# Mamba-2 block and FFN on one core: own decays on four row groups, past decays split into two factors, y between the two projections

## The chip, the core and the metric

The kernel is one program on one core of one Trainium2 chip. The metric is the device time of one execution in microseconds. Six engines are named by the profile: PE (TensorE matmuls), PEld (TensorE weight loads), DVE (VectorE), ACT (ScalarE), POOL (GpSimd) and SP (SyncE, which here only issues DMAs). They run their own instruction streams in order and meet through semaphores.

## The reference, cut to what matters

The input is x of shape (4, 256, 512). Two residual blocks follow each other: a Mamba-2 block (in-projection, causal convolution of length 4, a decayed attention-like sum over two chunks of 128 tokens, gate, group norm, out-projection) and a quantised FFN. The change lies in the first:

```python
# b=4 batches, s=256 tokens, chunks of 128; H=128 heads of P=64; G=8 groups; N=128; K=4
gate, hBC, dt = split(layernorm(x) @ in_proj_w.T)        # 8192 | 8192+2*1024 | 128
hBC = silu(causal_conv(hBC) + conv_b)                    # hs (8192), Bm (8*128), Cm (8*128)
dt  = clip(softplus(dt + dt_bias), 0, 100);  A = -exp(A_log)
xch = hs * dt                                            # per head
A_cum = cumsum(dt * A) within a chunk
L = exp(segsum(dt * A))                                  # L[l,s] = exp(A_cum[l]-A_cum[s]), s <= l
Y_diag = einsum(C, B, L, xch)                            # a chunk on itself ("own")
states = einsum(B, exp(A_cum[last] - A_cum), xch)        # left behind by a chunk
Y_off  = einsum(C, states of the chunk before, exp(A_cum))   # second chunk on the first ("past")
y = Y_diag + Y_off + hs * D
g = y * silu(gate);  out = groupnorm(g) * norm_w @ out_proj_w.T
```

With two chunks per batch, each head needs three decay matrices of 128x128 per batch: chunk 0 on itself, chunk 1 on the past chunk 0, chunk 1 on itself.

## The kernel before

The 1024 tokens lie on the free axis. The 8192 channels are 64 tiles of 128 channels (two heads each), eight tiles per group. `step(g, j, par_, ...)` exists once for every engine and does tile j of group g; `over_tiles` runs it 64 times, with two parities `par_`, and after each eight tiles `window(g, nxt)`, which projects the next group's B and C, multiplies them (`cbs`), takes the group norm's sums and does the out-projection of the group. The FFN (`over_chunks`) comes last. Inside a step TensorE also projects the channels of the NEXT tile, in four units `unit(0)` to `unit(3)`: inputs for tokens 0 to 511 and 512 to 1023, then gate for the same halves. A unit is twelve matmuls of 512 columns (fp32 split into an upper and a lower part, L758 to L760). `unit` waits on `split` (weights ready) and `taken` (the bank of the unit before is read out).

What TensorE does in a step before: `turn(0)` (four transposes of the tile's inputs, L858), `exponents(0)`, `exponents(1)`, `unit(0)`, `turn(1)`, `exponents(2)`, `exponents(3)`, `unit(1)`, `y_first` (8 matmuls, L881), `exponents(4)`, `exponents(5)`, `unit(2)`, `unit(3)`, `y_second` (16 matmuls, L891). `exponents(q)` (L867) is one bf16 matmul over rows of three exact parts of the cumulative sums; it leaves A_cum[l]-A_cum[s] for one kind (q // 2: own 0, past, own 1) and one head (q % 2) in one of three PSUM banks (`diff0`, `diff1`, `misc`).

ScalarE turns these into decays: Relu with scale -1 and Exp with scale -1 for the own kinds (L640, L644), a plain Exp for the past (L634). VectorE multiplies with C·B (`weigh`, L1163, into M), multiplies the transposed inputs with dt (`times_dt`, L1155), runs the last three taps of the convolution (`conv_rest`, L1068), the silu products (`hs_silu` L1082, `gate_silu` L1087), and adds y to the skip term (L1189, which signals `ysum`). ScalarE also does the first tap (`tap3`, L558), the tanh of inputs (`hs_tanh`, L569) and gate (`gate_tanh`, L573), the rounding of the raw weights to their upper part (`upper_pair`, L536, waits for `s_raw`), and scale and rounding of the out-projection's weights (L666, L672). GpSimd makes the lower parts (L406, L430), gated = y * gate (L438), its squares (L447) and their sum (L452). SP loads, per step, the raw out-projection weights (`wo_raw`), the rows of the next tile (`load_rows`, one DMA of `row_r` and three of `row_l`), and two raw weight pieces (`load_pair`).

The order on each engine is the order in which the code is written; nothing reorders it. The same small pool of PSUM banks (two `proj`, two `diff`, two `y`, `trb`, `misc`) ties the engines together.

Of the kernel before, what the change touches and what calls it, by code (L numbers as in the profile page):

```python
# [5 lines left out]
F32 = mybir.dt.float32  # L6
F32R = mybir.dt.float32r
BF16 = mybir.dt.bfloat16
ALU = mybir.AluOpType
# [20 lines left out]
UNITS = 6  # L30
SLOT = [0, 1, 2, 3, 0, 1]
# [18 lines left out]
def over_tiles(eng, step, window):  # L50


    with eng.Fori(0, G - 1) as g:
        with eng.Fori(0, TPG // 2) as p:
            step(g, 2 * p, 0, True, True)
            step(g, 2 * p + 1, 1, True, True)
        window(g, True)
    with eng.Fori(0, TPG // 2 - 1) as p:
        step(G - 1, 2 * p, 0, True, True)
        step(G - 1, 2 * p + 1, 1, True, True)  # L60
    step(G - 1, TPG - 2, 0, True, False)
    step(G - 1, TPG - 1, 1, False, False)
    window(G - 1, False)
# [12 lines left out]
def mamba_ffn(nc, x, win, wdt, par, parbc, dt_bias, a_log, wout, w1, w3, w2, s1, s3, s2, out):  # L76
    rows_r = nc.dram_tensor("rows_r", (3, H, TOK), BF16, kind="Internal").ap()
    rows_l = nc.dram_tensor("rows_l", (3, B, H, 3, P), BF16, kind="Internal").ap()

    with ExitStack() as ctx:  # L80
# [23 lines left out]
        M = sb("M", [P, 4, HALF])  # L104
        bc = M[:, :, :].rearrange("p (a u) f -> p a (u f)", a=2)
# [3 lines left out]
        row_r = sb("row_r", [P, 2, 2, TOK], BF16)  # L109
        row_l = sb("row_l", [P, 2, 2, 3 * P], BF16)  # L110
        sq = sb("sq", [P, 2, HALF])
        after, bias_bc, nega_bc = [sq[:, 0, i * P:(i + 1) * P] for i in range(3)]
# [12 lines left out]
        qs = sb("qs", [P, 2, 4])  # L125
        qr = sb("qr", [P, 2, 4])
# [9 lines left out]
        rev, revrem = dte[:, 0:HALF], dte[:, HALF:TOK]  # L136
        r_part = flat[:, 4 * TOK:6 * TOK].bitcast(BF16)[:, 0:3 * TOK].rearrange("p (k f) -> p k f", k=3)
        neg_part = flat[:, 6 * TOK:8 * TOK].bitcast(BF16)[:, 0:3 * TOK].rearrange("p (k f) -> p k f", k=3)
        rev_part = pre[0].bitcast(BF16)[:, 0:3 * HALF].rearrange("p (k f) -> p k f", k=3)
# [3 lines left out]
        f_pair = M[:, :, :].rearrange("p k (w f) -> p w k f", w=2)  # L143
# [27 lines left out]
        dbank = diff + [misc]  # L171
# [32 lines left out]
        s_part = [sem(f"exact_part{k}") for k in range(3)]  # L204
        s_rest = sem("rest_of_parts")
        s_rows = sem("rows_stored")
        s_raw = [sem("w_raw0_loaded"), sem("w_raw1_loaded")]
        s_rowq = [sem("rows_even_loaded"), sem("rows_odd_loaded")]
        s_out = sem("out_stored")
# [10 lines left out]
        turned = Tally(sem("hs_transposed"), 0, 2)  # L220
        xdts = Tally(sem("xdt_done"), 1, 2)
        dready = Tally(sem("diff_ready"), 0, UNITS)
        dbound = Tally(sem("diff_bounded"), 0, 4)
        edone = Tally(sem("exp_done"), 0, UNITS)
        mdone = Tally(sem("decay_done"), 3, UNITS)
        yready = Tally(sem("y_ready"), 1, 3)
# [47 lines left out]
        def _(sp):  # L274
# [12 lines left out]
            for n in range(3):  # L287
                load_pair(n, 2 * n if n else None)

            def load_rows(t, par_):  # L290
                sp.dma_start(row_r[0:3, par_, :, :], rows_r[:, bass.ds(2 * t, 2), :]).then_inc(s_rowq[par_], 16)
                for k in range(3):
                    sp.dma_start(row_l[3 + 4 * k:7 + 4 * k, par_, :, :].rearrange("b h f -> b (h f)"),
                                 rows_l[k, :, bass.ds(2 * t, 2), :, :].rearrange("b h q f -> b (h q f)"))\
                        .then_inc(s_rowq[par_], 16)


            for k in range(3):
                sp.wait_ge(s_part[k], 3)
                sp.dma_start(rows_r[k, :, :], r_part[:, k, :]).then_inc(s_rows, 16)  # L300
                sp.dma_start(rows_l[k, :, :, 1, :].rearrange("b h l -> h b l"),
                             rev_part[:, k, :].rearrange("h (b l) -> h b l", b=B)).then_inc(s_rows, 16)
                for z in range(2):
                    sp.dma_start(rows_l[k, :, :, 2 * z, :].rearrange("b h l -> h b l"),
                                 neg_part[:, k, :].rearrange("h (b z l) -> h z b l", z=2, b=B)[:, z, :, :])\
                        .then_inc(s_rows, 16)
            sp.wait_ge(s_const, 13)
            sp.dma_start(row_r[3:15, 0, 1, :], row_r[3:15, 0, 0, :]).then_inc(s_marks, 16)
            sp.dma_start(row_r[3:15, 1, 0, :], row_r[3:15, 0, 0, :]).then_inc(s_marks, 16)
            sp.dma_start(row_r[3:15, 1, 1, :], row_r[3:15, 0, 0, :]).then_inc(s_marks, 16)  # L310
            sp.wait_ge(s_rows, 16 * 12)
            load_rows(0, 0)

            def step(g, j, par_, nxt, nxt2):
# [39 lines left out]
        def _(pool):  # L354
# [18 lines left out]
            e.memset(row_r[:, :, :, :], 0.0).then_inc(s_const, 1)  # L373
            e.memset(row_l[:, :, :, :], 0.0).then_inc(s_const, 1)
            pool.wait_ge(s_const, 9)
            e.memset(row_l[0:3, :, :, :], 1.0).then_inc(s_const, 1)
            columns = row_r[:, 0, 0, :].rearrange("p (b f) -> p b f", b=B)
            for k in range(3):
                pool.wait_ge(s_const, 10 + k)
                e.affine_select(out=columns, in_=columns, compare_op=ALU.not_equal, fill=1.0, base=-3 - 4 * k,  # L380
                                pattern=[[-1, B], [0, S]], channel_multiplier=1).then_inc(s_const, 1)
# [31 lines left out]
            split_pair(0, 0)  # L413
            split_pair(1, 2)

            wholes = ((acum, rem, r_part), (rev, revrem, rev_part))
            for i, (whole, rest, parts) in enumerate(wholes):
                pool.wait_ge(s_part[0], i + 1)
                e.tensor_tensor(rest, whole, parts[:, 0, :], ALU.subtract).then_inc(s_rest, 1)
            for i, (whole, rest, parts) in enumerate(wholes):  # L420
                pool.wait_ge(s_rest, i + 1)
                pool.wait_ge(s_part[1], i + 1)
                e.tensor_tensor(parts[:, 2, :], rest, parts[:, 1, :], ALU.subtract).then_inc(s_part[2], 1)
            split_pair(1, 4)

            def step(g, j, par_, nxt, nxt2):
# [15 lines left out]
                for h in range(2 if nxt else 0):  # L442
                    pool.wait_ge(gdone.sem, gdone.at(g, j, h + 1))
# [907 lines left out]
```

## Time and profile before

| | us |
|---|---|
| median of 3 runs | 1861.39 (1861.02 to 1861.64) |
| the profiled execution | 1863.36 |
| its span on the core | 1861.6 |
| PE busy | 1805.1 (97%) |
| DVE busy | 1256.5 (67%) |
| POOL busy | 1006.2 (54%) |
| ACT busy | 918.5 (49%) |
| mean granted TensorE clock | 0.986 of full speed |

The span is what the core's trace covers; 1.8 us of the profiled execution lie around it, and that execution is 1.97 us above the median. The matmuls' ends are modelled, so that a busy PE is no proof that the array has no gaps: the chain of waits is read for that.

### The profile page before, as it was taken

Reading aid. Unit: us, or ns where it says so; the run is one execution under the profiler, and the core shown is the slowest. Engines: PE = TensorE matmul, PEld = TensorE weight load, DVE = VectorE, ACT = ScalarE, POOL = GpSimd, SP = SyncE. Lnnn points to the kernel's source line nnn. Section 1 sums busy time; section 2 is a strip of 40 time slices with the busy share of each in tenths; the row PEclk is TensorE's granted clock in tenths of the full one; section 3 lists DMA queues with packets and bytes.
Section 4 is the critical chain, followed back from the end, with each engine's and each line's share of the span. In section 5 each row is a group of like instructions: output and inputs, shape, how many; then the busy total and the mean of one; then the engine's idle time right before and its main releaser. Section 6 shows DMA issues by size and latency. Waiting matters only on the chain.

```text
span 1861.6 us, 35838 instructions
## 1 busy us (share of the span) xinstructions
PE 1805.1 (97%) x10520; PEld 1448.8 (78%) x10520; DVE 1256.5 (67%) x2147; ACT 918.5 (49%) x1660; POOL 1006.2 (54%) x812
## 2 busy tenths in 40 slices
PE   5799999999999999999999999999999998999998
PEld 4577887788777877787778777887788776788886
DVE  6588728872887377746884688457754884877776
ACT  4466526652665256635663566346644663222221
POOL 4266645664566446654665366546654657633430
PEclk9899999999999999999999999999999997999999
DMA  2211101110111011101120111001101111111101
GB/s 93 63 53 41 46 3 45 52 52 0 47 53 52 0 47 51 53 0 36 46 64 6 29 53 53 17 29 53 47 23 30 42 35 53 40 52 35 51 17 46
DMA packets 49019, 74.94 MB, mean 40 GB/s; under 512 B 10356, under 2 KB 18676, under 8 KB 48984
## 3 DMA queue, kind: packets, MB, share of 16 engines
q1 hardware_dynamic: 47976, 73.12, 12.9%
q10 hardware_dynamic: 1008, 1.38, 0.2%
q8 instruction: 18, 0.29, 0.1%
q14 instruction: 17, 0.14, 0.0%
HBM read 70.35 MB, written 4.06 MB: 40 GB/s over the span
## 4 chain that ended last, share of the span: by engine, by line
PE 94%; DVE 2%; POOL 1%; issue 1%; ACT 1%; POOLq 0%; DVEq 0%; ACTq 0%
PE proj L758 16%; PE proj L760 16%; PE proj L759 16%; PE y L891 7%; PE y L945 6%; PE y L947 6%; PE y L946 6%; PE y L881 4%; PE trb L858 3%; PE diff L867 3%; PE y L758 2%; PE y L760 2%; PE y L759 2%; PE misc L867 1%; PE misc L931 1%
## 5 line engine op out<-in xcount | busy, mean ns | idle before, releaser
L758 PE MATMUL proj<-xhi,w_hi 128*128 128x512 f32 x1088 | 466.1, 428 | 5.4 <-DVE v L1068 5.4
L760 PE MATMUL proj<-xhi,w_lo 128*128 128x512 f32 x1088 | 426.2, 392 | 0.0
L759 PE MATMUL proj<-xlo,w_hi 128*128 128x512 f32 x1088 | 425.5, 391 | 0.0
L406 POOL TENSOR_TENSOR w_lo<-w_raw,w_hi 128x512 fp32r<-128x512 f32 x144 | 184.1, 1297 | 227.5 <-ACT w_hi L536 227.5
L1068 DVE SCALAR_TENSOR_TENSOR v<-proj,par_sb,v 128x510 f32<-128x510 f32 (+2 forms) x384 | 282.1, 742 | 14.9 <-ACT v L558 11.6
L758 PEld LDWEIGHTS proj<-xhi,w_hi 128*128 128x128 f32 x1088 | 205.0, 188 | 75.5 <-issue 7.9
L462 POOL TENSOR_TENSOR g_lo<-gated,g_hi 128x512 fp32r<-128x512 f32 x128 | 163.8, 1283 | 182.1 <-ACT g_hi L689 182.0
L760 PEld LDWEIGHTS proj<-xhi,w_lo 128*128 128x128 f32 x1088 | 204.8, 188 | 46.5
L759 PEld LDWEIGHTS proj<-xlo,w_hi 128*128 128x128 f32 x1088 | 205.4, 189 | 38.6
L1163 DVE TENSOR_TENSOR M<-diff,cb 128x512 f32<-128x512 f32 x256 | 170.4, 686 | 82.2 <-ACT diff L644 82.2
L945 PE MATMUL y<-wo_hi,g_hi 128*128 128x512 f32 x512 | 202.9, 396 | 4.0 <-POOL g_lo L462 4.0
L430 POOL TENSOR_TENSOR wo_lo<-wo_raw,wo_hi 128x512 f32 (+1 forms) x64 | 81.9, 1279 | 225.1 <-ACT wo_hi L672 225.1
L946 PE MATMUL y<-wo_lo,g_hi 128*128 128x512 f32 x512 | 200.1, 391 | 0.0
L947 PE MATMUL y<-wo_hi,g_lo 128*128 128x512 f32 x512 | 200.0, 391 | 0.0
L689 ACT CAST g_hi<-gated 128x512 fp32r<-128x512 f32 x128 | 78.6, 620 | 233.6 <-PE y L947 233.6
L558 ACT ACTIVATE v<-proj,par_sb 128x512 f32<-128x512 f32 x128 | 99.6, 778 | 188.7 <-PE proj L760 188.7
L1207 DVE SCALAR_TENSOR_TENSOR resid<-y,rg,resid 128x512 f32<-128x512 f32 x64 | 48.0, 750 | 201.3 <-PE y L947 171.5
L640 ACT ACTIVATE diff<-diff 128x512 f32<-128x512 f32 x192 | 105.5, 579 | 138.1 <-PE diff L867 138.1
L438 POOL TENSOR_TENSOR gated<-hs,gate 128x512 f32 (+1 forms) x128 | 162.8, 1295 | 1.6 <-DVE hs L1189 1.6
L452 POOL TENSOR_TENSOR sqacc<-sqacc,sq 128x512 f32<-128x512 f32 x128 | 163.1, 1297 | 0.0
L891 PEld LDWEIGHTS y<-M,xdt 128*64 128x64 f32 x2048 | 112.0, 138 | 25.7 <-issue 22.2
L891 PE MATMUL y<-M,xdt 128*64 128x128 f32 x2048 | 127.6, 278 | 2.5 <-DVE M L1163 2.5
(179 smaller groups left out, 3420.1 us busy)
## 6 DMA issues: line engine op xcount, KB each, us to landing
w_raw<-in_win SPq DMA_DIRECT2D x144, 256.0 KB, 2.7
wo_raw<-in_wout SPq DMA_DIRECT2D x64, 256.0 KB, 2.6
M<-in_w SPq DMA_DIRECT2D x14, 512.0 KB, 3.7
cb<-in_w SPq DMA_DIRECT2D x7, 512.0 KB, 3.4
row_l<-rows_l SPq DMA_DIRECT2D x192, 6.0 KB
out<-resid SPq DMA_DIRECT2D x8, 256.0 KB, 2.0
rows_l<-gated SPq DMA_DIRECT2D x9, 128.0 KB, 2.5
resid<-in_x SPq DMA_DIRECT2D x4, 256.0 KB, 4.7
```

Source lines behind the costliest of these rows:

```text
L406: e.tensor_tensor(w_lo[:, slot, i, :], w_raw[:, i, :], w_hi[:, slot, i, :].bitcast(F32), ALU.subtract).then_inc(split.sem, 1)
L452: e.tensor_tensor(halves(sqacc, h), halves(sqacc, h), sq[:, h, :], ALU.add)\
L462: e.tensor_tensor(g_lo[:, kk, :, :], gated[:, 4 * kk:4 * kk + 4, t * P:(t + 1) * P], g_hi[:, kk, :, :].bitcast(F32), ALU.subtract).then_in ...
L758: e.matmul(o, hi_l, hi_r, start=first, stop=False)
L759: e.matmul(o, hi_l, lo_r, start=False, stop=False)
L760: return e.matmul(o, lo_l, hi_r, start=False, stop=last)
L891: mm = e.matmul(ybank[b // 2][head * HD:(head + 1) * HD, (b % 2) * S + P:(b % 2 + 1) * S], xdt[:, 2 * b + part, head * HD:(head + 1) * HD] ...
L945: e.matmul(o, g_hi[:, kk, k, :], wo_hi[:, kt, :], start=first, stop=False)
L946: e.matmul(o, g_hi[:, kk, k, :], wo_lo[:, kt, :], start=False, stop=False)
L947: mm = e.matmul(o, g_lo[:, kk, k, :], wo_hi[:, kt, :], start=False, stop=last)
L1068: e.scalar_tensor_tensor(dst[:, :, d:S], src[:, :, 0:S - d], weights(K - 1 - d), dst[:, :, d:S], ALU.mult, ALU.add)\
L1163: e.tensor_tensor(M[:, SLOT[q], :], dbank[q % 3][:, :], cb[:, q // 2, :], ALU.mult)\
```

## The change

Tiles, projections, window and FFN stay as they are. What changes:

- **Own exponents.** The rows of z (0, 1: own kinds) and head go to four groups of 15 partitions, at 0, 32, 64 and 96 (`first = 32 * (2 * z + head)`). `exponents(g, j, par_)` issues four matmuls of 512 columns, each contracting its own 15 rows, into the four banks of `decay[0]` and `decay[1]`. ScalarE and VectorE then work on two banks at once (1024 columns): two Relu, two Exp, two products per step in place of four, four and four.
- **Past decays.** No exponent matmul and no Exp any more. exp(A_cum[l]) is made once for all heads (`faded`, in DRAM) and loaded per tile as `fade_l` by two DMAs that broadcast a row to 128 partitions; GpSimd multiplies it with C·B into M[:, 4:6] (`weigh_past`, 1024 columns). The other factor, `fade_s` = exp(sum after s) * dt, is multiplied into a second copy of the transposed inputs, `xfade`, by VectorE.
- **Order.** A step starts with `unit(0)`, then all eight transposes in one go into the two y banks, `unit(1)`, all 24 matmuls of `y`, `exponents` of the NEXT tile, `unit(2)`, `unit(3)`. ScalarE's weight casts (`upper_pair`) move ahead of the second first tap, the out-projection's weights ahead of the decays, and the next tile's decays stand among the tanhs; VectorE adds y before the last silu products. The exponents of a group's first tile move into the window.
- **Rows.** `load_rows` issues eight DMAs (3 or 12 rows each) in place of four; `load_fade` adds two of 256 KB, behind a wait for `weigh_past`.
- **Start.** B and C of group 0 are projected first, then inputs and gate of tile 0; there are two cumulative products as before, fewer exact parts (three per head in place of nine).
- `sq` has one buffer in place of two.

On TensorE, from the products of y to the gate's unit, in the loop over tiles. `row_r` and `row_l` are the rows and columns of an exponent matmul, `xdt` the inputs times dt. Before:

```order
L881 MATMUL y<-M,xdt 64x128 x8
L867 MATMUL diff<-row_r,row_l 128x512
L865 REGISTER_ALU
L867 MATMUL misc<-row_r,row_l 128x512
L795 REGISTER_ALU
L797 REGISTER_ALU
L758 MATMUL proj<-xhi,w_hi 128x512
```

Now, at the same place:

```order
L929 MATMUL y<-M,xdt 64x128 x4
L929 MATMUL y<-M,xfade 64x128 x2
L929 MATMUL y<-M,xdt 64x128 x2
L889 ISA
L890 ISA
L891 ISA
L895 MATMUL decay<-row_r,row_l 128x512 x4
L830 REGISTER_ALU
L832 REGISTER_ALU
L794 MATMUL proj<-xhi,w_hi 128x512
```

The third of y that stood here is now the whole of it, followed by one set of four exponents for the next tile instead of two of the six for this one.

On ScalarE, from the weight casts to the inputs' second tanh. `w_hi` are the upper parts of the weights. Before:

```order
L536 CAST w_hi<-w_raw 128x512 x2
L639 REGISTER_ALU
L640 ACTIVATE diff<-diff 128x512
L639 REGISTER_ALU
L640 ACTIVATE misc<-misc 128x512
L643 REGISTER_ALU
L644 ACTIVATE diff<-diff 128x512
L643 REGISTER_ALU
L644 ACTIVATE misc<-misc 128x512
L569 ACTIVATE hs<-v 128x512
```

Now the casts stand ahead of the second first tap, and these rows follow the inputs' first tanh:

```order
L689 ACTIVATE wo_raw<-wo_raw,par_sb 128x512
L693 ISA
L693 COPY wo_hi<-wo_raw 128x512
L660 ISA
L661 ACTIVATE decay<-decay 128x1024
L601 ACTIVATE hs<-v 128x512
L660 REGISTER_ALU
L661 ACTIVATE decay<-decay 128x1024
L666 ACTIVATE decay<-decay 128x1024
L604 REGISTER_ALU
L605 ACTIVATE gate<-proj 128x512
L666 ACTIVATE decay<-decay 128x1024
```

The decays of the next tile are spread between the tanhs; the Exp of the second pair of banks stands between the two gate tanhs.

The diff, cut to its core:

```diff
-        sq = sb("sq", [P, 2, HALF])
+        row_r = sb("row_r", [P, 2, HALF], BF16)
+        row_l = sb("row_l", [P, 2, P], BF16)
+        fade_l = sb("fade_l", [P, 2, HALF])
+        fade_s = sb("fade_s", [P, B, H])
+        xfade = sb("xfade", [P, B, P])
+        sq = sb("sq", [P, HALF])
...
-        diff = [bank("diff0"), bank("diff1")]
-        ybank = [bank("y0"), bank("y1")]
-        trb = bank("trb")
-        misc = bank("misc")
+        decay = [ctx.enter_context(nc.psum_tensor(f"decay{z}", [P, 2 * HALF], F32)) for z in range(2)]
+        diff = [decay[0][:, 0:HALF], decay[0][:, HALF:2 * HALF]]
+        ypair = ctx.enter_context(nc.psum_tensor("y", [P, 2 * HALF], F32))
+        ybank = [ypair[:, 0:HALF], ypair[:, HALF:2 * HALF]]
+        misc, trb = decay[1][:, 0:HALF], decay[1][:, HALF:2 * HALF]
...
 # SP
                 if nxt:
-                    sp.wait_ge(dready.sem, dready.at(g, j, 1))
+                    sp.wait_ge(dready.sem, dready.at(g, j, 0))
                     load_rows(TPG * g + j + 1, 1 - par_)
+                    sp.wait_ge(pdone.sem, pdone.at(g, j, 1))
+                    load_fade(TPG * g + j + 1)
                 if nxt2:
                     load_pair(9 * g + j + 3, split.at(g, j, 0))
...
 # GpSimd
+            def weigh_past(g, j):
+                pool.wait_ge(s_fade, (32 * TPG) * g + 32 * j + 32)
+                pool.wait_ge(cbd.sem, cbd.at(g, 0, 0))
+                pool.wait_ge(yready.sem, yready.at(g, j, 0))
+                e.tensor_tensor(M[:, 4:6, :], fade_l[:, :, :], cb[:, 1:2, :].broadcast_to([P, 2, HALF]), ALU.mult)\
+                    .then_inc(pdone.sem, 1)
...
+                if ahead:
+                    weigh_past(g, j + 1)
...
 # ScalarE
                 if nxt:
                     tap3(0, w, ready.at(g, j, 1), silu.at(g, j, -1))
-                decay(2)
-                decay(3)
+                if nxt2:
+                    act.wait_ge(ready.sem, ready.at(g, j, 0))
+                    upper_pair(par_, 9 * g + j + 3)
                 if nxt:
                     tap3(1, w, ready.at(g, j, 2), silu.at(g, j, 0))
                     act.wait_ge(gdone.sem, gdone.at(g, j, 0))
                     hs_tanh(hs[:, 1 - par_, :], 0, taken.at(g, j, 1))
...
+                if ahead:
+                    bounded(g, j + 1, 0)
+                if nxt:
+                    hs_tanh(hs[:, 1 - par_, :], 1, taken.at(g, j, 2))
+                if ahead:
+                    bounded(g, j + 1, 1)
+                    exponential(g, j + 1, 0)
+                if nxt:
+                    gate_tanh(gate[:, 1 - par_, :], 0, ready.at(g, j, 3))
+                if ahead:
+                    exponential(g, j + 1, 1)
+                if nxt:
+                    gate_tanh(gate[:, 1 - par_, :], 1, ready.at(g, j, 4))
...
 # TensorE
+            def exponents(g, j, par_):
+                pe.wait_ge(mdone.sem, mdone.at(g, j, 0))
+                pe.wait_ge(s_rowq[par_], (TPG * 64) * g + 64 * j + (128 - 64 * par_))
+                pe.wait_ge(cbd.sem, cbd.at(g, 0, 0))
+                for z in range(2):
+                    for head in range(2):
+                        first = 32 * (2 * z + head)
+                        mm = e.matmul(decay[z][:, head * HALF:(head + 1) * HALF],
+                                      row_l[first:first + PARTS + PARTS * B, par_, :],
+                                      row_r[first:first + PARTS + PARTS * B, par_, :], start=True, stop=True)
+                    mm.then_inc(dready.sem, 1)
...
-                turn(0)
-                exponents(0)
-                exponents(1)
                 if nxt:
                     unit(0)
-                turn(1)
-                exponents(2)
-                exponents(3)
+                turn()
                 if nxt:
                     unit(1)
-                y_first()
-                exponents(4)
-                exponents(5)
+                y()
+                if ahead:
+                    exponents(g, j + 1, 1 - par_)
                 if nxt:
                     unit(2)
                     unit(3)
-                y_second()
...
 # VectorE
+            def weigh_own(g, j, z):
+                dve.wait_ge(edone.sem, edone.at(g, j, z + 1))
+                dve.wait_ge(yready.sem, yready.at(g, j, 0))
+                e.tensor_tensor(M[:, 2 * z:2 * z + 2, :], decay[z][:, :].rearrange("p (a f) -> p a f", a=2),
+                                cb[:, 2 * z:2 * z + 1, :].broadcast_to([P, 2, HALF]), ALU.mult)\
+                    .then_inc(mdone.sem, 1)
...
                 w = tile_weights(t + 1)
-                times_dt(0)
-                weigh(0)
-                weigh(1)
-                times_dt(1)
+                times_dt()
...
+                if nxt:
+                    hs_silu(hs[:, 1 - par_, :], 1, tanh.at(g, j, 2))
+                if ahead:
+                    weigh_own(g, j + 1, 0)
+                if nxt:
+                    gate_silu(gate[:, 1 - par_, :], 0, tanh.at(g, j, 3))
+                if ahead:
+                    weigh_own(g, j + 1, 1)
+                if nxt:
+                    gate_silu(gate[:, 1 - par_, :], 1, tanh.at(g, j, 4))
```

`ahead` is false in the last step of a group, where the next tile's exponents and decays stand at the end of the window instead.

## Rows read from the trace of the kernel before

**Rows 1.** The page: busy time and share of each engine, and the chain.

```profile
PE 1805.1 (97%) x10520; PEld 1448.8 (78%) x10520; DVE 1256.5 (67%) x2147; ACT 918.5 (49%) x1660; POOL 1006.2 (54%) x812
PE 94%; DVE 2%; POOL 1%; issue 1%; ACT 1%; POOLq 0%; DVEq 0%; ACTq 0%
```

**Rows 2.** Windows: stretch, its us, busy us of each engine, PEclk, DMA share, GB/s.

```profile
0.00:81.69 81.69, 49.35 (x209) 39.84 (x209) 48.02 (x69) 34.49 (x49) 31.11 (x34) 0.87 0.27 79
81.69:100.14 18.45, 16.77 (x112) 12.85 (x112) 14.19 (x22) 10.93 (x20) 3.11 (x3) 1.00 0.15 45
512.76:529.11 16.35, 16.35 (x112) 12.90 (x114) 13.26 (x20) 10.93 (x20) 10.85 (x9) 1.00 0.16 50
98.24:289.12 190.88, 190.31 (x1162) 152.55 (x1164) 125.97 (x189) 103.54 (x186) 111.17 (x91) 1.00 0.13 38
1534.56:1552.69 18.13, 8.68 (x62) 5.94 (x63) 7.26 (x12) 8.69 (x16) 13.88 (x13) 0.63 0.07 20
```

**Rows 3.** Chain of waits from 512.76: start, us, what (x counts weight loads too).

```profile
512.76 1.90 PE y L891 x32
514.65 0.59 PE trb L858 x4
515.67 0.23 PE proj L758
...
518.42 0.44 PE trb L858 x4
...
522.04 1.02 PE y L881 x16
523.07 0.32 PE diff L867
523.39 0.21 PE misc L867
```

**Rows 4.** Groups of instructions by line and form: count, busy us, mean ns, idle before.

```profile
L1068 DVE SCALAR_TENSOR_TENSOR v<-proj,par_sb,v 128x510 f32<-128x510 f32 x128 | 95.7, 747 | 12.6 <-ACT v L558 11.6
L569 ACT ACTIVATE hs<-v 128x512 f32<-128x512 f32 x128 | 81.2, 635 | 18.4 <-DVE v L1068 17.6
L666 ACT ACTIVATE wo_raw<-wo_raw,par_sb 128x512 f32<-128x512 f32 x64 | 47.1, 736 | 0.0
L577 ACT ACTIVATE gated<-gated 128x1024 f32<-128x1024 f32 x1 | 1.1, 1062 | 1.5 <-DVE gated L1104 1.5
L1114 DVE SCALAR_TENSOR_TENSOR gated<-gated 128x1024 f32<-128x1024 f32 x1 | 1.2, 1217 | 0.0
L452 POOL TENSOR_TENSOR sqacc<-sqacc,sq 128x512 f32<-128x512 f32 x128 | 163.1, 1297 | 0.0
L419 POOL TENSOR_TENSOR gated<-gated 128x1024 f32<-128x1024 f32 x1 | 2.1, 2127 | 37.5 <-ACT gated L609 37.5
```

**Rows 5.** Timeline of one step: start, us, engine, line, operation, tiles, count.

```profile
515.49 1.07 ACT L640 ACTIVATE diff<-diff 128x512 f32<-128x512 f32 x2 [1.59 <-PE diff L867]
...
516.68 1.27 SPq L293 DMA_DIRECT2D row_l<-rows_l  x3
...
517.09 1.29 DVE L1163 TENSOR_TENSOR M<-diff,cb 128x512 f32<-128x512 f32 x2 [0.82 <-ACT diff L644]
...
518.30 0.98 SPq L285 DMA_DIRECT2D w_raw<-in_win  x2
```

**Rows 6.** DMA issues: tiles, queue, count, KB each, median us to landing.

```profile
w_raw<-in_win SPq DMA_DIRECT2D x144, 256.0 KB, 2.7
gated<-in_wdt SPq DMA_DIRECT2D x1, 256.0 KB, 6.6
```

**Rows 7.** Timeline of the start, engines DVE and PE.

```profile
45.13 1.22 DVE L1119 SCALAR_TENSOR_TENSOR gated<-dt,sq 128x1024 f32<-128x1024 f32 x1
...
76.43 0.77 PE L840 MATMUL diff<-M 128*128 128x128 f32 x2 [11.14 <-DVE M L1082]
...
81.69 0.63 PE L858 MATMUL trb<-ident,hs 128*128 128x128 f32 x4
```

More of the change, by code:

```diff
@@ L124, in mamba_ffn @@
         rg = sb("rg", [P, TT])
[L125 to L126 removed]
+        qs, qr = [fade_s[:, i, 0:2 * KD].rearrange("p (a n) -> p a n", a=2) for i in range(2)]
         flat = gated[:, :, :].rearrange("p a f -> p (a f)")
@@ new lines, in _ @@
+            sp.wait_ge(s_fade_l, 2)
+            sp.dma_start(faded, faded_sb).then_inc(s_faded, 16)
+            for k in range(PARTS):
+                sp.wait_ge(s_part[k], 1)
+                for z in range(2):
+                    sp.dma_start(rows[:, z, k, :, :],
+                                 parts[:, k, :].rearrange("h (b z l) -> h z b l", b=B, z=2)[:, z, :, :])\
+                        .then_inc(s_rows, 16)
+            sp.wait_ge(s_faded, 16)
+            load_fade(0)
+            sp.wait_ge(s_rows, 32 * PARTS)
@@ L312, in _, with step @@
             load_rows(0, 0)
-            def step(g, j, par_, nxt, nxt2):
+            def step(g, j, par_, nxt, nxt2, ahead):
                 sp.wait_ge(wolo.sem, wolo.at(g, j, 0))
@@ L411, in split_pair, with step @@
                     split_piece(slot, i, parts)
[L413 to L423, printed above, removed]
-            split_pair(1, 4)
-            def step(g, j, par_, nxt, nxt2):
+            split_pair(1, 0)
+            split_pair(0, 2)
+            pool.wait_ge(s_part[0], 1)
+            e.tensor_tensor(rem, acum, parts[:, 0, :], ALU.subtract).then_inc(s_rest[0], 1)
+            pool.wait_ge(s_rest[0], 1)
+            pool.wait_ge(s_part[1], 1)
+            e.tensor_tensor(parts[:, 2, :], rem, parts[:, 1, :], ALU.subtract).then_inc(s_part[2], 1)
+            split_pair(1, 4)
+            def weigh_past(g, j):
[4 more added lines that the diff above has]
+                    .then_inc(pdone.sem, 1)
+            weigh_past(0, 0)
+            def step(g, j, par_, nxt, nxt2, ahead):
                 if nxt2:
@@ L648, in step, with exponential, decays @@
+            def exponential(g, j, z):
+                act.wait_ge(dbound.sem, dbound.at(g, j, z + 1))
+                e.activation(decay[z][:, :], decay[z][:, :], ACT.Exp, scale=-1.0).then_inc(edone.sem, 1)
+            def decays(g, j):
+                bounded(g, j, 0)
+                bounded(g, j, 1)
+                exponential(g, j, 0)
+                exponential(g, j, 1)
+            decays(0, 0)
+            def step(g, j, par_, nxt, nxt2, ahead):
                 w = tile_weights(TPG * g + j + 1)
@@ L827, in _ @@
             for b in range(B):
-                mm = e.matmul(misc[:, b * P:(b + 1) * P], dta[:, 2 * b * P:(2 * b + 1) * P],
-                              after, start=True, stop=True)
+                mm = e.matmul(misc[:, b * P:(b + 1) * P], after, dta[:, 2 * b * P:(2 * b + 1) * P],
+                              start=True, stop=True)
             mm.then_inc(s_cum, 1)
@@ L879, in y_first @@
                     for b in range(B):
[L880 to L889 removed]
+                        cols = slice(b * P, (b + 1) * P)
@@ L954, in window @@
                         turn_x(n2, t - 2, hs[:, t % 2, 0:HID])
+                    if i == 13 and nxt:
+                        exponents(g + 1, 0, 0)
             over_tiles(pe, step, window)
@@ L1115, in _ @@
             link(e.scalar_tensor_tensor(dtq, dtv, 0.0, dtq, ALU.max, ALU.add))
+            for h in range(2):
+                hs_silu(bc[:, 0, :], h, h + 1)
             dt_flat = dt[:, :, :].rearrange("p t f -> p (t f)")
```

389 lines of the change are left out of this document (179 added, 210 removed).

## The prediction, made before the changed kernel had run

> **What bounds the kernel now.** The first page says that PE is busy for 97% of the span and holds 94% of the chain that ended last [rows 1]; the other engines are far from full. So only two things can move the time: work taken from TensorE, and waits that TensorE gets. The windows by stage, read next, show where it waits already [rows 2]: in a normal step of 16.35 us not at all, in eight steps with their window for 0.6 us of 190.9, but in the first 81.7 us for 32, and in the 18.1 us at the end of the last tile for over 9, at a granted clock of 0.87 and 0.63. The chain within one step [rows 3] gives TensorE's prices: a unit of twelve matmuls 2.75 us (515.67 to 518.42), four transposes 0.44, 16 matmuls of y 1.90, eight of them 1.02, an exponent matmul 0.21, and 0.32 behind y. What follows y is dearer by 0.11 (exponent) and 0.15 (transposes: 0.59 against 0.44).
>
> **TensorE's own work in a changed step.** Four units: 11.0. Eight transposes, now behind a unit: 2 x 0.44 = 0.88. 24 matmuls of y together: 1.90 and eight more at the margin, 1.90 - 1.02 = 0.88, so 2.78. Four exponent matmuls instead of six, each on 15 rows of its own: no row shows four on separate rows. Together at once they cost no less than one behind y, 0.32; one after the other 0.32 + 3 x 0.21 = 0.95. I take 0.45, near the low end, with one more change of shape before the next unit (0.11 to 0.15, as above). Sum 11.0 + 0.88 + 2.78 + 0.45 = 15.11, at most 15.61, against 16.35 before.
>
> The Trainium skill ("TensorEngine Tiling (Array Packing)", Key Properties) says that tiles on different rows run in parallel but that changing the tiling mode drains the array. The trace agrees with the second half as far as the 0.11 and 0.15 go; no run here shows the first. "TensorE: Matmul & The Clock Gate" (Measured speedup vs the span model) gives 3.07 times for four row tiles; by it the four cost an estimated 4 x 0.21 / 3.07 = 0.27 plus the changes of shape, about 0.5.
>
> **The chain through the other engines.** TensorE may now be faster than what feeds it. The decays of the next tile are made in the same step, behind ScalarE's other work, and VectorE's product stands ahead of `gate_silu` of half 0, for which the next `unit(0)` waits. I follow it from the start of `unit(0)` at 0. Widths of 1024 are priced by rows 4: 1.06 on ScalarE, 1.22 on VectorE; an instruction starts about 0.09 before the end of the one ahead if it doesn't depend on it (two in 1.29 and in 1.07, [rows 5]).
> - Transposes end at 3.63; with a handover (about 0.2 behind the array's modelled end) `times_dt` runs from 3.85, 1.22 + 0.69 less two overlaps: 5.58. Three dependent convolution taps of 0.75 and their signals: 7.9.
> - ScalarE: tanh of inputs, half 0, 0.64, then scale (0.74) and rounding (as a tanh, 0.64) of the out-projection's weights: free at 9.78. The exponents end at 9.16 + 0.45 = 9.6, so ScalarE, not TensorE, is late. Relu on two banks 0.94: 10.72.
> - Meanwhile VectorE: first tap of half 1 to 8.57, silu (behind the tanh) to 9.3, two taps to 10.75. The second tanh starts at 10.8, free at 11.34. Relu 12.28, Exp done 13.32.
> - VectorE, which has added y and made the second silu by 12.7, runs the product (1.22) and `gate_silu` (0.69): 15.2; with the signal `unit(0)` may start at 15.3.
>
> TensorE alone would need 15.11, so the chain ends last, by a little. It has some fourteen handovers, each counted at 0.04 to 0.05; for what is missed I take 15.4. Bounds: 15.11 (chain shorter than TensorE's work) to 16.0 (another 0.05 at each).
>
> **What is covered.** y waits for `times_dt` (5.7) and starts at 6.4. GpSimd gains `weigh_past`: 1024 columns, between 2.13 (the wide row of GpSimd) [rows 4] and 2 x 1.30; its 10.85 us in a step become 13.0 to 13.4 of 15.4. It makes gated from 11.4 to 14.0, `weigh_past` to about 16.5, that is 1.1 into the next step, where y wants it at 6.4; squares and sums end at 5.7, the weights' lower parts at 8.3, ahead of 9.8, when the next weights come. If that cover were gone, y would wait by the excess. SP issues eight row DMAs at 0.42 (three in 1.27, [rows 5]), needed nine microseconds later. Behind its new wait for `weigh_past` (1.1) stand two broadcasts and the two raw weight pieces, 0.49 each: the last piece is issued at 2.6 and lands 2.7 later [rows 6], at 5.3. `upper_pair`, which now stands ahead of the second first tap, may have it as late as 6.4 before conv half 1 moves.
>
> **The sum**, against the profiled execution of 1863.36:
> - 56 steps that make decays: 16.35 - 15.4 = 0.95 each, 53.2.
> - 7 last steps of a group, without exponents and without that chain: 11.0 + 0.88 + 2.78 = 14.66, so 1.69 each, 11.8. Seven windows get the exponents instead: -3.2.
> - The first step lost 2.1 on a normal one [rows 2]. It will still wait for its first decays (four wide passes of ScalarE and two products behind the first exponents), an estimated 1.4: 0.7.
> - The start. Before, C·B was multiplied at 76.43, after 11.1 us of waiting for B and C, and step 0 began at 81.69 [rows 7]. Now B and C come first: VectorE ends dt times A at about 50 instead of 46.35 (three taps and two silus more ahead), then needs C, the inputs of tile 0, and some 4 us in which ScalarE reads the cumulative sums: C·B at 64, and with its 5.3 us and the masks 71.3. The rows must be stored and loaded by then, eight DMAs: step 0 at 73. Gain 8.7; bounds 0 (the rows come through DRAM late) and 14.
> - The last tile: the exponents and decays are made before it, so between its last unit and the group norm's sum stand only transposes, `times_dt`, y, the additions, and GpSimd's leftovers: about 13 instead of 18.1 [rows 2]. Gain 5.
>
> 53.2 + 11.8 - 3.2 + 0.7 + 8.7 + 5 = 76.2, which gives 1787. The median of the runs is 2.0 below the profiled execution, so 1785.
>
> **Rivals.**
> 1. The four exponent matmuls run one after the other. For it: before, each bf16 matmul of 512 columns costs 0.21 whatever it contracts [rows 3], and nothing in the trace shows two at once on different rows. TensorE then needs 15.61 a step: 56 x 0.21 + 7 x 0.5 = 15 more, 1800. The two pages named above speak against it.
> 2. Instructions over two banks cost two of one bank. For it: the wide rows are all on SBUF [rows 4]. Three ScalarE passes at 2 x 0.58 instead of 0.94, 0.94 and 1.04 (0.56 in all) and two VectorE ones at 2 x 0.69 instead of 1.22 (0.3): 15.4 + 0.86, 48 more, 1833. Against it: both engines' time per column is the same in rows 4 and 5 once the fixed part is taken off.
> 3. Slower than before: the raw weights come late. SP holds them behind `weigh_past` and two broadcasts; ScalarE waits in `upper_pair` with the second tap, the tanhs and the decays queued behind it, VectorE's convolution behind those, and TensorE's `unit(0)` at the end. Each microsecond past 6.4 into the step is one per step, in 63 steps. The gain is used up at 76 / 63 = 1.2, so from a landing at 7.6, 5.0 after issue; with the 6.6 that a piece of the same size took among others at the start [rows 6] it lands at 9.2: 2.8 x 63 = 176 more, 1961. Against it: 2.7 is the median of 144, and the burst of a megabyte comes at a moment when the DMA engines are otherwise at 0.16 of their time [rows 2]. The skill's "DMA: Bandwidth & Descriptors" (Anatomy of one DMA) fits 2.0 us and 436 GB/s; by it a burst of four is done an estimated 4.4 after its first issue, at 5.5.
> 4. The steps come as forecast, but start and end give nothing (rows late, GpSimd's queue at the end): 14 more, 1799.
>
> **How the numbers follow.** Forecast 0.63, by itself 1769 to 1805 (0.29 less per step is -16; 0.35 more is +20). Rival 1 0.14, rival 2 0.08, rival 3 0.06, rival 4 0.09. The range reaches over rivals 1 and 4 and to the chain's upper bound of 16.0 (+34): 1766 to 1822. It leaves out most of rival 2 and rival 3. A measurement of this kernel tells a change of 0.2% (3.7 us) from none. Faster takes all but rival 3 and a sliver at its threshold: 0.93; same 0.02; slower 0.05.
>
> **What would show it.** In the changed profile: the step's period near 15.4; a short idle time of PE ahead of `unit(0)` put down to `gate_silu` (right) or none at a period near 15.6 (rival 1); four exponent matmuls within about 0.3 of one another; wide ScalarE passes near 1.0 and products near 1.2; no wait of ScalarE's weight casts for a DMA (rival 3 if there is); PE first in step 0 near 73; the group norm's sum about 13 after the last unit. The prediction is wrong if the period stays above 16.0, or if TensorE waits for GpSimd's `weigh_past`.

## The result, and the profile after

The changed kernel takes 1877.5 us (median of 4 runs, 1876.3 to 1878.0) against 1861.2 in the same series: a ratio of 1.009, 95% interval 1.007 to 1.010. It is slower by 16 us, where 1785 was forecast. The profiled execution's span is 1876.1 us at a mean clock of 0.992.

First the page of the changed kernel: busy time and share of each engine, against [rows 1].

```profile
PE 1750.3 (93%) x10392; PEld 1407.7 (75%) x10392; DVE 1263.9 (67%) x1892; ACT 840.9 (45%) x1273; POOL 1184.9 (63%) x873
```

TensorE did lose 55 us of work, but it now idles 126 us instead of 56.5. The windows say where, the same three places as in [rows 2] (stretch, its us, busy us per engine, PEclk, DMA share, GB/s):

```profile
0.00:67.21 67.21, 44.53 (x212) 35.95 (x213) 47.57 (x73) 30.84 (x47) 24.23 (x32) 0.97 0.30 91
511.85:528.97 17.12, 15.63 (x109) 12.30 (x109) 13.39 (x17) 9.76 (x14) 13.73 (x11) 1.00 0.28 78
1550.00:1567.70 17.70, 9.43 (x75) 8.27 (x73) 8.90 (x11) 7.51 (x12) 16.20 (x13) 0.81 0.11 29
```

The first unit of step 0 starts at 67.21, where before the first transposes did at 81.69: 14.5 us are gained. The last unit ends at 1553.88; from there to the end are 322.2 us, against 327.0 from 1534.56 before: 4.8 gained. The stretch between lasts 1486.7 instead of 1452.9: 33.8 lost. The three add up to the 14.5 us by which the two spans differ. So the loss lies in the steps: this one lasts 17.12 us, not 16.35, and not the 15.4 of the forecast. Over all of them, from one tile's y to the next tile's within a group, it is 16.05 us for the first of each group and 17.16 in the mean for those behind it. Where a run below has a step, it is that second mean.

What waits in them is in the table of waits (engine, line, waited for: us in total, times, longest):

```profile
ACT w_hi L568 <- DMA w_raw<-in_win: 171.8, 58, 3.7
PE proj L794 <- DVE gate L1116: 76.9, 62, 1.6
POOL gated L467 <- DVE hs L1222: 51.0, 63, 1.0
```

TensorE waits for `gate_silu`, as foreseen. But behind that stands ScalarE, which waits 3 us in each step for the raw weights. The DMA issues of the same kernel (tiles, queue, count, KB, median us to landing), against 2.7 in [rows 6]:

```profile
w_raw<-in_win SPq DMA_DIRECT2D x144, 256.0 KB, 4.2
fade_l<-faded SPq DMA_DIRECT2D x128, 256.0 KB, 3.7
```

And the lines by form, against [rows 4] (the silu products of the inputs were L1082 before and L1111 now, gated was L438 and is L467):

```profile
L1111 DVE SCALAR_TENSOR_TENSOR hs<-hs,v 128x512 f32<-128x512 f32 x128 | 167.0, 1305 | 1.1
L1188 DVE TENSOR_TENSOR M<-decay,cb 128x1024 f32<-128x1024 f32 x128 | 154.3, 1211 | 1.0 <-ACT decay L666 1.0
L450 POOL TENSOR_TENSOR M<-fade_l,cb 128x1024 f32<-128x1024 f32 x64 | 152.9, 2389 | 2.7 <-issue 2.7
L467 POOL TENSOR_TENSOR gated<-hs,gate 128x512 f32 x96 | 142.8, 1508 | 37.5 <-DVE hs L1222 37.5
```

The wide product costs the foreseen 1.21, `weigh_past` 2.39. `hs_silu`, an instruction that nobody touched, takes 1.31 in the mean and took 0.69 before. The 1.51 of gated is a mean of two kinds: the first of each pair takes 1.29, and the second 1.72 wherever a silu runs beside it (63 of 64 steps). Its shortest, median and longest, in ns:

```profile
L467 POOL TENSOR_TENSOR gated<-hs,gate x128: 1266/1299/1749, 82.2 to 1563.0; 128x512 f32 x96, 128x512 f32<-128x512 f32 x32
```

The timeline of one step, from its `unit(0)` at 511.84 to the next at 528.97, in the order of what released what (start, us, engine, line, count, idle time and releaser):

```profile
513.70 0.90 SPq L315 DMA_DIRECT2D fade_l<-faded  x2
514.91 0.93 SPq L297 DMA_DIRECT2D w_raw<-in_win  x2
519.15 1.31 ACT L568 CAST w_hi<-w_raw 128x512 fp32r<-128x512 f32 x2 [3.05 <-DMA w_raw<-in_win]
520.37 0.77 ACT L590 ACTIVATE v<-proj,par_sb 128x512 f32<-128x512 f32 x1
521.17 0.75 DVE L1097 SCALAR_TENSOR_TENSOR v<-proj,par_sb,v 128x510 f32<-128x510 f32 x1 [1.03 <-ACT v L590]
521.84 1.09 DVE L1111 SCALAR_TENSOR_TENSOR hs<-hs,v 128x512 f32<-128x512 f32 x1
522.85 1.52 DVE L1097 SCALAR_TENSOR_TENSOR v<-proj,par_sb,v 128x508 f32<-128x508 f32 x2
524.28 1.40 DVE L1222 SCALAR_TENSOR_TENSOR hs<-hs,par_sb,y 128x512 f32<-128x512 f32 x2
525.34 2.97 POOL L467 TENSOR_TENSOR gated<-hs,gate 128x512 f32 x2 [0.82 <-DVE hs L1222]
525.60 1.58 DVE L1111 SCALAR_TENSOR_TENSOR hs<-hs,v 128x512 f32<-128x512 f32 x1
...
528.27 2.39 POOL L450 TENSOR_TENSOR M<-fade_l,cb 128x1024 f32<-128x1024 f32 x1
...
530.82 0.90 SPq L315 DMA_DIRECT2D fade_l<-faded  x2
```

This is a closed loop, and TensorE isn't in it. SP issues broadcasts and weights when `weigh_past` is done; ScalarE casts the weights when they land; behind the casts stands the second first tap, behind that VectorE's taps, behind those the additions of y; GpSimd's gated waits for these, and `weigh_past` stands behind gated. From start to start: 1.21 (broadcasts issued), 4.24 (landing), 1.22 (casts), 0.80 (tap), 4.17 (VectorE up to gated's start), 2.93 (gated), 2.55 (`weigh_past` and its signal): 17.12, the step's period. The first step of a group stands outside it, with the 16.05 above: its `weigh_past` is run in the window, so that its casts don't wait (at 465.7, for example).

### The profile page after: what moved, and what is told of

Its sections match the earlier page's. It is cut to its first block and busy times, and to the rows that moved or that the text cites. A ratio compares the mean times of both kernels' runs of the same rounds, so it can differ in the third digit from the quotient of the medians.

```text
span 1876.1 us, 34372 instructions
## 1 busy us (share of the span) xinstructions
PE 1750.3 (93%) x10392; PEld 1407.7 (75%) x10392; DVE 1263.9 (67%) x1892; ACT 840.9 (45%) x1273; POOL 1184.9 (63%) x873
## 5 line engine op out<-in xcount | busy, mean ns | idle before, releaser
L794 PE MATMUL proj<-xhi,w_hi 128*128 128x512 f32 x1080 | 447.2, 414 | 80.8 <-DVE gate L1116 76.9
L1097 DVE SCALAR_TENSOR_TENSOR v<-proj,par_sb,v 128x510 f32<-128x510 f32 x378 | 279.9, 742 | 72.5 <-ACT v L590 51.7
L467 POOL TENSOR_TENSOR gated<-hs,gate 128x512 f32 (+1 forms) x128 | 190.0, 1506 | 51.0 <-DVE hs L1222 51.0
L1205 DVE TENSOR_TENSOR xdt<-y,dt 128x1024 f32<-128x1024 f32 x64 | 78.3, 1224 | 142.1 <-PE y L913 142.1
L929 PE MATMUL y<-M,xdt 128*64 128x128 f32 x2048 | 170.9, 277 | 2.6 <-DVE xfade L1209 2.6
L1111 DVE SCALAR_TENSOR_TENSOR hs<-hs,v 128x512 f32<-128x512 f32 x128 | 167.0, 1305 | 1.1
L568 ACT CAST w_hi<-w_raw 128x512 fp32r<-128x512 f32 x144 | 87.8, 619 | 173.4 <-DMA w_raw<-in_win 171.8
L1188 DVE TENSOR_TENSOR M<-decay,cb 128x1024 f32<-128x1024 f32 x128 | 154.3, 1211 | 1.0 <-ACT decay L666 1.0
```

The lines of the kernel that those rows point to most:

```text
L467: e.tensor_tensor(gated[:, bass.ds(j, 1), h * HALF:(h + 1) * HALF], hs[:, par_:par_ + 1, h * HALF:(h + 1) * HALF], gate[:, par_:par_ + 1, ...
L794: e.matmul(o, hi_l, hi_r, start=first, stop=False)
L929: mm = e.matmul(ybank[b // 2][head * HD:(head + 1) * HD, (b % 2) * S + z * P:(b % 2) * S + (z + 1) * P], inputs[:, head * HD:(head + 1) * ...
L1097: e.scalar_tensor_tensor(dst[:, :, d:S], src[:, :, 0:S - d], weights(K - 1 - d), dst[:, :, d:S], ALU.mult, ALU.add)\
L1111: e.scalar_tensor_tensor(halves(dst, h), halves(dst, h), 1.0, v[:, h, :], ALU.add, ALU.mult)\
```

## The experiments

Every kernel is the changed one with the edit shown. Times are medians, with the ratio to the kernel before and its 95% interval.

**Raw weights first (e1).** Theory A: the late weights are the loss. Theory B: `hs_silu`, slow beside GpSimd, is.

```diff
+                if nxt2: load_pair(...)
                 sp.wait_ge(pdone.sem, pdone.at(g, j, 1))
                 load_fade(TPG * g + j + 1)
-                if nxt2: load_pair(...)
```

> The changed kernel with one move on SP: the two raw weight pieces are issued behind the row DMAs and ahead of the wait for weigh_past and of the two broadcasts. Theory A (the weight pieces come late, ScalarE's casts hold the second first tap, and by VectorE's convolution and gate_silu this reaches unit(0)): ScalarE's 172 us of waiting for w_raw go, the step falls from 17.1 to about 15.6, the time to about 1795. Theory B (VectorE's instructions with both operands in SBUF run at 1.55 us beside GpSimd instead of 0.69, and that makes the chain long): w_raw's wait goes, but the step stays at 16.5 or more, 1845 or more. Theory C (the four wide passes of ScalarE and its order are the bound): no change of the time, TensorE waits as long for gate_silu.

1808.95 us, 0.972 (0.970 to 0.973), step 15.88; of the casts' wait for the DMA 2.8 us are left. Late weights are worth 68.5 us. Theory A holds, though 14 us above its 1795; B as the main cause and C fall.

**Small broadcasts (e2).** SP's order and its wait stay; the two broadcasts carry an eighth of the columns.

```diff
-            def load_fade(t):
+            def load_fade(t, cols=HALF):
-                    sp.dma_start(fade_l[:, head, :], faded[bass.ds(2 * t + head, 1), :]
+                    sp.dma_start(fade_l[:, head, 0:cols], faded[bass.ds(2 * t + head, 1), 0:cols]
...
-                    load_fade(TPG * g + j + 1)
+                    load_fade(TPG * g + j + 1, 64)
```

> The changed kernel with its order of issue, but each of the two broadcasts per step carries 64 of its 512 columns (the past decay of most tokens is left at that of the first tile). It parts theory A in two. A1, the transfer: the broadcasts' 512 KB ahead of the weights delay their landing (4.2 us against 2.7 before); then landing falls to about 2.9, the second piece is there at about 6.4 instead of 7.7 into the step, the step is near 16.0 and the time about 1820. A2, the order: what matters is when the pieces are issued (3.1 and 3.6 into the step); then landing changes little and the time stays within 10 us of 1877.

1838.77 us, 0.988 (0.986 to 0.989), step 16.47. The table of DMA issues of this run:

```profile
w_raw<-in_win SPq DMA_DIRECT2D x144, 256.0 KB, 3.5
```

The landing is 0.7 shorter (3.5 for 4.2), and the step by the same 0.69 (16.47 for 17.16): in this loop, a leg's saving comes out whole. The result lies between the two expectations (1820, and within 10 of 1877): the landing fell to 3.5, not to the 2.9 that A1 took. So 39 of the 68 us hang on the size of the broadcasts, and by difference the rest on where the weights are issued.

**Casts moved back (e3)** behind the inputs' first tanh on ScalarE; the weights are as late as in the changed kernel.

```diff
-                if nxt2: upper_pair(par_, 9 * g + j + 3)
                 if nxt:
                     tap3(1, ...); hs_tanh(..., 0, ...)
+                if nxt2: upper_pair(par_, 9 * g + j + 3)
```

> The changed kernel with the weight casts of ScalarE where they stood before, behind the inputs' first tanh; SP as in the changed kernel. Theory A: the pieces (7.7 into the step) are there when the casts come, the second first tap is no longer held (6.5 instead of 8.5), but the two casts (1.15 us) now lie between the tanh and the next tile's decays: step near 16.6, time about 1850. Theories B and C: as C·B and decays come later by the casts, the step grows by up to 1 us: 1900 or more, or no change.

1855.41 us, 0.996 (0.995 to 0.998), step 16.7, as theory A had it (16.6, 1850). The casts wait for the DMA for only 3.8 us in all, and TensorE waits 72.8 us for `gate_silu` all the same. The decays are late instead, in this run's waits:

```profile
DVE M L1188 <- ACT decay L666: 42.6, 56, 0.9
```

ScalarE's two casts, 1.13 us, now stand ahead of them; in the changed kernel that wait is 1.0 us in all.

**Second silu ahead of the additions of y (e4)**, with the weights first.

```diff
+                hs_silu(hs[:, 1 - par_, :], 1, tanh.at(g, j, 2))
                 for h in range(2): ... halves(y, h) ...   # the two additions
-                hs_silu(hs[:, 1 - par_, :], 1, tanh.at(g, j, 2))
```

> As e1, and on VectorE the inputs' second silu stands ahead of the two additions of y (whose first releases GpSimd's gated), so that it no longer runs beside GpSimd. Theory B as a part of the price: the silu takes 0.69 instead of 1.5, its start waits some 0.5 us for the tanh, the step is 0.1 to 0.3 shorter than in e1: 5 to 15 us faster than e1. Without an effect of GpSimd on VectorE it is 0.1 to 0.6 us a step slower than e1, since VectorE waits for the tanh.

1850.24 us, 0.994 (0.992 to 0.995): 41 us worse than with the weights first alone (step 16.67), so the expectation missed in sign. The second silu took 0.69 now; but the first had moved beside GpSimd's `w_lo`, where 54 of them took 1.56 in the mean, and TensorE waited 64.9 us for `gate_silu`.

**The same with short squares on GpSimd (e6)**: squares and sums on 64 of 512 columns.

```diff
-  one = gated[..., h * HALF:(h + 1) * HALF];  e.tensor_tensor(sq[:, :], one, one, ALU.mult)
+  one = gated[..., h * HALF:h * HALF + 64];   e.tensor_tensor(sq[:, 0:64], one, one, ALU.mult)
```

> The kernel e4 (1850 us; there the first silu of the inputs takes 1.46 to 1.56 us beside GpSimd's lower parts of the weights) with GpSimd's squares and their sums cut from 512 to 64 columns each (most of the group norm's sum is left out). GpSimd is then about 4 us earlier at the weights' lower parts and done with them before the silu. Theory: GpSimd slows VectorE's instructions that read only SBUF, and that alone costs e4 its 41 us on e1. Then the silu falls to 0.69, the step from 16.67 to 15.8 or less, the time to 1800 or less. Rival: what e4 lost is VectorE's wait for the tanh (0.7 us a step); then the step stays above 16.5 and the time above 1840.

1800.96 us, 0.968 (0.966 to 0.969), step 15.8. GpSimd comes to `w_lo` earlier, and no silu meets it. The line by form:

```profile
L1112 DVE SCALAR_TENSOR_TENSOR hs<-hs,v 128x512 f32<-128x512 f32 x128 | 88.6, 692 | 51.4 <-ACT hs L602 44.0
```

All 128 are back at 0.69, and 49 us with them, though VectorE's own program is that of the run before. The rival falls: VectorE's wait for the tanh is 44.0 us here and was 44.0 in e4 too. GpSimd has up to 4.6 us less to do per step as well (2 x 1.04 and 2 x 1.28, now short), so the 49 are both: fewer meetings, and a GpSimd that is earlier.

**Transposes first (e7)**, with the weights first:

```diff
-                if nxt: unit(0)
                 turn()
-                if nxt: unit(1)
+                if nxt: unit(0); unit(1)
```

> The kernel e1 (1809 us) with the eight transposes at the start of the step, ahead of unit(0), as four of them were in the kernel before. The chain from the transposes over times_dt and the convolution to gate_silu starts 2.8 us earlier, and the transposes fill the time in which unit(0) waits. Theory: with the weights in time, what is left of TensorE's idle time is this chain; the step falls from 15.87 to TensorE's own 15.5, some 20 us, less up to 7 for the wait for the last addition at each group's start: 1790 to 1800. Rival: the chain is ScalarE's wide passes and their order from the exponents on (these don't move): no change from 1809, or slower.

1778.35 us (1777.0 to 1779.2), 0.956 (0.954 to 0.957): 4.4% faster than the kernel before, the best of all, and below the 1790 to 1800 expected. The page of this run and its transposes, three steps running (15.1 to 15.2 apart):

```profile
PE 1722.4 (97%) x10392; PEld 1415.7 (80%) x10392; DVE 1265.3 (71%) x1892; ACT 843.1 (47%) x1273; POOL 1195.7 (67%) x873
```

```profile
495.15 1.04 PE L914 MATMUL y<-ident,hs 128*128 128x128 f32 x8
510.27 1.03 PE L914 MATMUL y<-ident,hs 128*128 128x128 f32 x8
525.43 1.03 PE L914 MATMUL y<-ident,hs 128*128 128x128 f32 x8
```

TensorE's wait for `gate_silu` is 2.5 us in all; it is the bound again, as before the change. The slow silus are still there (its second one takes 1.58 in 63 steps) and cost nothing: they are covered.

**The same, all four exponents on the first 15 rows (e8)** (the decays of the other kinds and heads are replaced by the first's).

```diff
-                        first = 32 * (2 * z + head)
+                        first = 0
```

> The kernel e7 with all four exponent matmuls on the first 15 rows (the decays of the other kinds and heads are replaced by those of the first). What the four row groups are worth by themselves: in the trace of the changed kernel four matmuls take 0.32 us together. If that is because they run at once, here they take 0.3 + 3 x 0.21 = 0.95, 0.6 a step more, and where TensorE is the bound 35 to 40 us more than e7. If 15 rows alone make them cheap, nothing changes.

1813.39 us, 0.974 (0.973 to 0.976), 35 more, as expected. TensorE's timeline, first with four row groups, then with one:

```profile
519.53 0.40 PE L896 MATMUL decay<-row_r,row_l 15*128 15x512 bf16 x4
519.86 0.50 PE L795 MATMUL proj<-xhi,w_hi 128*128 128x512 f32 x1
```

```profile
516.88 1.03 PE L896 MATMUL decay<-row_r,row_l 15*128 15x512 bf16 x4
517.85 0.50 PE L795 MATMUL proj<-xhi,w_hi 128*128 128x512 f32 x1
```

From the exponents' start to the next unit's, 0.33 against 0.97: on rows of their own the four run side by side.

**Transposes first, weights late as in the changed kernel (e9).**

```diff
-                if nxt: unit(0)
                 turn()
-                if nxt: unit(1)
+                if nxt: unit(0); unit(1)
```

> The changed kernel with y's transposes at the start of the step, ahead of the inputs' unit, as in the run at 1778 us, but with the raw weights issued where the changed kernel issues them, behind the wait for weigh_past and behind the two broadcasts. Theory A (the late raw weights bind by themselves): they still land about 7 us into a step and the second half's first tap still ends near 9, so the second silu ends some 16.5 into the step and holds the next one; a step of 16.3 to 16.9 us, 1825 to 1865 us in all, and the wait of the cast for w_raw stays some 3 us. Theory C (only y's late start held the step, and the order of SP's issues matters only because of it): a step of 15.2 to 15.4, 1778 to 1795 us.

1880.43 us, 1.010 (1.008 to 1.012). TensorE's order, worth 31 us with the weights first (1808.95 to 1778.35), is worth nothing here, and theory C falls. Theory A's direction held, its 1825 to 1865 did not: I had let the step follow from the tap's time within it. The waits of this run:

```profile
ACT w_hi L568 <- DMA w_raw<-in_win: 166.8, 57, 3.5
POOL gated L467 <- DVE hs L1221: 52.7, 63, 1.0
```

They are those of the changed kernel, and that a change of TensorE's order left the step near 17.1 (17.0, 17.4 and 17.1 in three running) points to a loop without TensorE, theory D. The first step of each group, ahead of which no step's loop stands, takes 15.11 in this run; those behind it take 17.08.

**`weigh_past` ahead of gated on GpSimd (e10).** Everything else, SP's order too, stays.

```diff
+                if ahead: weigh_past(g, j + 1)
                 for h in range(2): ... gated ...
-                if ahead: weigh_past(g, j + 1)
```

> The changed kernel with one instruction moved on GpSimd: weigh_past of the next tile stands ahead of gated, not behind it. SP's order stays: wait for weigh_past, two broadcasts, then the raw weights; TensorE's, ScalarE's and VectorE's orders stay too. Theory D (a closed loop without TensorE sets the 17.12 us: weigh_past, issue and landing of the raw weights 5.6 us, casts 1.3, second first tap 0.8, VectorE's taps and silu to the additions of y 4.2, gated 3.0 and weigh_past 2.4): the loop is cut, since weigh_past no longer waits for the additions; it ends at about 15.0 into the step instead of 18.8, the weights are issued some 3.7 us earlier and land before ScalarE wants them; no wait of the cast for w_raw, a step of 15.9 to 16.4 and 1809 to 1842 us, slower than with the weights issued first by what gated, now 1.6 us later, costs. Theory A as it stood (the two broadcasts ahead of the weights and their landing cost what they cost): 39 of the 68 us stay, about 1850.

1853.02 us, 0.995 (0.994 to 0.997), step 16.6 to 16.8: over theory D's range. Its cause was right: the casts' wait fell from 171.8 us to 43.2. Its price was not, and the timeline shows why.

```profile
ACT w_hi L568 <- DMA w_raw<-in_win: 43.2, 58, 2.6
```

```profile
515.77 2.38 POOL L450 TENSOR_TENSOR M<-fade_l,cb 128x1024 f32<-128x1024 f32 x1
518.12 2.97 POOL L469 TENSOR_TENSOR gated<-hs,gate 128x512 f32 x2
```

```profile
516.33 2.37 DVE L1111 SCALAR_TENSOR_TENSOR hs<-hs,v 128x512 f32<-128x512 f32 x1
518.62 1.21 DVE L1188 TENSOR_TENSOR M<-decay,cb 128x1024 f32<-128x1024 f32 x1
```

The silu now meets `weigh_past`, ends 0.55 after it, and has taken 2.37: 1.7 more than alone, right on the way to `unit(0)`. The total of 1853 is also what the other theory gave for its own reason (broadcasts and landing), so the time alone doesn't decide; the wait that went does.

**What the silu's time is made of.** Over all steps of the changed kernel, a silu that starts while GpSimd runs one of its products ends 0.55 us after that instruction's end: 63 beside the first gated (median 1.58 long), 54 beside `w_lo` (1.15). The 0.55 holds within 0.01 in every other trace in which a silu is held, beside `weigh_past` (2.37) and `wo_lo` (1.05, in e3) as well. With GpSimd idle at its start it takes 0.69. Both inputs of `hs_silu` lie in SBUF. VectorE's instructions with an input in PSUM don't change beside the same GpSimd work: L1188 takes 1210 ns when GpSimd runs all along and 1215 when it doesn't, and `gate_silu` takes 672, where it took 684 before with GpSimd idle. The Trainium skill ("SBUF — State Buffer", Who interferes with whom) has this rule: a VectorE instruction with two SBUF inputs and a GpSimd instruction that reads SBUF need the same port, and the later one is blocked for the whole of the other. The trace agrees in both directions. In the step above the silu, started 0.26 after the first gated, ends 0.55 behind it, so that 0.14 of its 0.69 lie outside the hold. The second gated, started while the silu still runs, takes 1.72 instead of 1.29.

## Why the prediction was wrong

- **The failed step is in "What is covered".** "the last piece is issued at 2.6 and lands 2.7 later [rows 6], at 5.3. `upper_pair`, which now stands ahead of the second first tap, may have it as late as 6.4 before conv half 1 moves." Measured in the step above: `weigh_past` ends 1.7 into the step instead of 1.1 (513.54), the weights are issued from 3.1 to 4.0, and the casts start at 7.3 and end at 8.6. The 2.7 was the landing with only small row loads ahead in the queue, and I used it for pieces behind half a megabyte; the same row reads 4.2 now. The burst of four, an estimated 4.4 us in rival 3, takes about 6.1 from its first issue (513.70) to its last piece's cast. The fit behind that estimate ("DMA: Bandwidth & Descriptors" in the Trainium skill, Anatomy of one DMA) is given for DMAs that GpSimd issues; these come from SP. That is rival 3, with a chance of 0.06. Its rule, one for one past 6.4, fits: the first piece is there at 7.3, the second some 0.6 later, so about 1.5 late in 63 steps gives 95 us, and 1787 + 95 = 1882. That it comes so near the measured 1878 is partly luck: with the weights first the kernel takes 1809, not 1787, and the late weights are worth 68.5, not 95; the two errors cancel.
- **What the step left out is that it closes a loop.** I followed the chain once, from TensorE's unit to the next, and took the end of `weigh_past` as given. It hangs on the additions of y, these on the taps, these on the casts, these on `weigh_past`. Whatever is late there comes back in the next step. Shown by e9, transposes first with late weights (no gain), and by e10, `weigh_past` moved (the casts' wait down from 171.8 to 43.2).
- **A second step failed beside it: VectorE's silu at 0.69.** I had priced it from rows in which GpSimd was idle beside it: before the change no silu overlapped a GpSimd instruction by more than 0.15. The change moved both. In the step above it costs 0.4 (first silu), 0.37 (gated, 2.97 for two instead of 2 x 1.30) and 0.9 (second silu, on the way to `unit(0)`). The first two lie on the loop of 17.12, the third doesn't.
- **The chain through the other engines (15.4)** was short by a little even without late weights: 15.88 with the weights first, inside its bounds (15.11 to 16.0). There the second silu still takes 1.58. With the transposes first the step is 15.11 in the median (15.25 in the mean), which is TensorE's own 15.11.
- **TensorE's own work**: four exponents to the next unit 0.32, inside my 0.45; rival 1 (one after another, 0.95) is what the one-row-group kernel shows, 0.97 and 35 us. "TensorEngine Tiling (Array Packing)" in the Trainium skill (Key Properties) has tiles on different rows run in parallel: these two runs agree.
- **Rival 2** fell: 1.0 and 1.21 on two PSUM banks.
- **Start**: 14.5 gained, 8.7 foreseen, just over my upper bound of 14: C·B at 59.75, not 64, and exponents at 66.51 after 2.4 us of waiting for the rows. **End**: 4.8 gained, 5 foreseen (13.8 from the last unit to the group norm's sum, 13 foreseen). Rival 4 fell.
- **The sum.** The stretch of steps was to get 62.5 shorter (53.2 + 11.8 - 3.2 + 0.7) and got 33.8 longer: a miss of 96. From one tile's y to the next's within a group it takes 17.0 in the mean of all, 1.6 more than 15.4: 90 us in 56 steps. From a group's last y over its last step and the window to the next group's first y it takes 76.3 in both kernels, where the two terms for it (1.69 and -0.45) promised 1.23 less: 9 us in seven. With the weights first it takes 75.2, so that this part, too, is the late weights. What little is left goes the other way.
- By the runs, in the whole time: late weights 68 us; the late start of y's chain behind `unit(0)` 31, seen only once the weights are early. The blocking of the silu is inside both and has no number of its own in the changed kernel: no run took it away alone.

## What to carry to other kernels

When a change adds a wait to a queue, ask not only what stands behind it but whether what it waits for comes back to it: a loop through SP, ScalarE, VectorE and GpSimd sets a period of its own, and here no order on the busiest engine changed it. A landing time read from a quiet queue (2.7 us here) is a lower bound for a transfer behind others (3.5 and 4.2). And moving an instruction of VectorE with both inputs in SBUF changes its price with what GpSimd does at that moment: lay the two timelines beside each other before counting it.

## What the runs showed of the hardware

- An unchanged silu of 128x512 took 0.69, 1.15, 1.58 or 2.37 us by the GpSimd instruction that it met, ending 0.55 after it each time. GpSimd's second gated, started beside it, took 1.72 instead of 1.29.
- Four bf16 matmuls of 15 rows and 512 columns on four row groups passed in 0.32 to 0.33 us up to the next unit's start, on one row group in 0.97.
- A 256 KB piece behind two 256 KB broadcasts landed 4.2 us after issue, behind two of 32 KB 3.5, ahead of them 2.7 (medians).
